# Two reorderings at the end of the couples' loop: one exponential a tanh later on ScalarE, one key product ahead of the turned gates on TensorE

## The reference

```python
# layer 2, cross attention (features = layernorm(x); textual_features = ctx)
h = jnp.tanh(txt_proj[:, None, :, :] + feat_proj[:, :, None, :] + b[None, None, :, :][..., 0, :])
rho = jnp.einsum('bftd,d->bft', h, w[:, 0])
att = jax.nn.softmax(rho + (1.0 - qm)[:, None, :] * NEG, axis=-1)
txt_h = jnp.einsum('bft,btd->bfd', att, textual_features)
w_s = jnp.tanh(jnp.einsum('bfd,od->bfo', txt_h, Wcw) + bcw)
b_s = jnp.tanh(jnp.einsum('bfd,od->bfo', txt_h, Wcb) + bcb)
x = x + jnp.tanh(g_xattn[2]) * (w_s * features + b_s)
# layer 2, experts: 16 of them, the 4 best of the 2 best groups
s = jax.nn.sigmoid(x2 @ Wg.T)
w = top4_in_best_groups(s)            # masked, normalised, times 2.5
y = y + (silu(x2 @ W1[e].T + b1[e]) * (x2 @ W3[e].T + b3[e]) @ W2[e].T + b2[e]) * w[e]
# layer 3, cross attention: keys K = ctx @ W_k.T, rotated
```

## Time and profile before

| | |
|---|---|
| median of 3 runs | 589.69 us (589.43 to 589.74) |
| profiled execution | 589.77 us, of which its span is 588.0 us |
| PE busy | 559.3 us (95%) |
| DVE busy | 441.0 us (75%) |
| ACT busy | 402.3 us (68%) |
| POOL busy | 101.9 us (17%) |
| mean granted TensorE clock | 0.994 of full speed |

### The profile page before, as it was taken

The page is one execution under the profiler, slowest core; times in us unless marked ns, Lnnn a source line. Parts: engine busy times, 40 slices in busy tenths (PEclk is TensorE's granted clock), DMA queues, the critical chain, the costliest instruction groups (busy, mean ns, idle before and its releaser), DMA issues.

```text
span 588.0 us, 8733 instructions
## 1 busy us (share of the span) xinstructions
PE 559.3 (95%) x3258; PEld 387.0 (66%) x3258; DVE 441.0 (75%) x692; ACT 402.3 (68%) x561; POOL 101.9 (17%) x69
## 2 busy tenths in 40 slices
PE   8999999898999999999996999999999999999997
PEld 5688787656767767765331346566546677888886
DVE  3377987868839799987889775766768828787786
ACT  3698899855856755426999865534504858888875
POOL 5400000000210000003999703200000310000000
PEclk8999999999999999999999899999999999999999
DMA  6118120300100369220000024506400100811100
GB/s 242 33 41 310 50 71 1 116 1 2 56 1 2 127 243 230 65 72 1 7 1 1 1 71 117 174 3 175 147 36 3 42 32 3 322 42 67 36 2 36
DMA packets 19342, 43.81 MB, mean 75 GB/s; under 512 B 2090, under 2 KB 7594, under 8 KB 19300
## 3 DMA queue, kind: packets, MB, share of 16 engines
q1 hardware_dynamic: 19300, 43.25, 22.7%
HBM read 42.55 MB, written 0.70 MB: 74 GB/s over the span
## 4 chain that ended last, share of the span: by engine, by line
PE 69%; DVE 15%; ACT 11%; issue 3%; POOL 1%; DVEq 0%; ACTq 0%; POOLq 0%
PE ps L820 36%; ACT work L1219 7%; PE ps L862 4%; PE ps L569 3%; PE ps L552 3%; DVE h_lo L1756 2%; PE ps L846 2%; PE ps L848 2%; PE ps L847 2%; PE ps L686 2%; PE ps L559 2%; PE ps L659 2%; PE ps L887 2%; PE ps L801 2%; DVE h_act L1729 2%
## 5 line engine op out<-in xcount | busy, mean ns | idle before, releaser
L1756 DVE TENSOR_TENSOR h_lo<-h_act,h_hi 128x512 fp32r<-128x512 f32 (+1 forms) x114 | 103.6, 913 | 39.7 <-ACT h_hi L1266 38.9
L820 PE MATMUL ps<-n_hi,w_hi 128*128 128x512 f32 x224 | 86.8, 422 | 2.4 <-DVE h_act L1729 1.2
L1266 ACT CAST h_hi<-h_act 128x1024 fp32r<-128x1024 f32 (+1 forms) x88 | 75.4, 857 | 14.6 <-PE ps L820 12.1
L820 PE MATMUL ps<-n_hi,w_lo 128*128 128x512 f32 x224 | 79.7, 391 | 0.0
L820 PE MATMUL ps<-n_lo,w_hi 128*128 128x512 f32 x224 | 79.6, 390 | 0.0
L1969 POOL TENSOR_TENSOR rstd<-var_eps,minus_half 128x4 f32<-128x4 f32 x16 | 17.2, 1075 | 312.1 <-DVE var_eps L1411 312.1
L1219 ACT ACTIVATE work<-work,p_rest 128x2048 f32<-128x2048 f32 x31 | 59.5, 2000 | 1.0 <-DVE work L1609 1.0
L1259 ACT ACTIVATE h_act<-ps 128x512 f32<-128x512 f32 x44 | 26.3, 598 | 45.6 <-PE ps L820 45.4
L820 PE MATMUL ps<-h_hi,w_hi 128*128 128x512 f32 x162 | 56.2, 395 | 0.1
L820 PE MATMUL ps<-h_hi,w_lo 128*128 128x512 f32 x162 | 55.3, 390 | 0.0
L820 PE MATMUL ps<-h_lo,w_hi 128*128 128x512 f32 x162 | 55.3, 390 | 0.0
(11 more groups left out here) (235 smaller groups left out, 1041.1 us busy)
## 6 DMA issues: line engine op xcount, KB each, us to landing
work<-g_rows SPq DMA_DIRECT2D x36, 512.0 KB, 5.8
w_f<-in_w SPq DMA_DIRECT2D x20, 512.0 KB, 3.7
w_f<-in_w SPq DMA_DIRECT2D x8, 384.0 KB, 3.2
work<-g_rows SPq DMA_DIRECT2D x8, 256.0 KB, 7.3
work<-g_rows SPq DMA_DIRECT2D x4, 384.0 KB, 7.2
diag<-in_w SPq DMA_DIRECT2D x2, 512.0 KB, 4.7
work<-in_w SPq DMA_DIRECT2D x2, 512.0 KB, 4.4
w_f<-in_w_rest SPq DMA_DIRECT2D x2, 384.0 KB, 4.6
```

The lines of the kernel that those rows point to most:

```text
L820: mm = pe.matmul(dst[i], wap(wt, e, lo, size, rows), mv[i], start=(first and c == 0), stop=(last and c == 2))
L1266: act.copy(places(h_hi, m, step), places(h_act, m, step)).then_inc(s["hi"], 1)
L1756: dve.tensor_tensor(lo, src, hi.bitcast(F32), ALU.subtract).then_inc(s["lo"], 1)
```

## The change

```diff
@@ TensorE, moe(m), if L == 2 @@
                         if g == 30:
                             pe.wait_ge(x2["sumA"], own_sums(2 * B - 1))
                             up(1)
+                    keep_busy(2, 4)
+                    prepare_keys(1, 1, 0)
                     turn_gates((0,))
-                    keep_busy(8, 4)
-                    prepare_keys(1, 1, 0)
                     pe.wait_ge(once["gT"], nth(m))
                     prepare_keys(1, 1, 1)
                     up(2)
@@ ScalarE, pair_sums @@
                     if g == 29:
                         norm_high(5, 0)
+                    if g == 30:
                         first_routing()
```

## The result

The changed kernel is slower: 592.11 us median of 22 runs, against 589.03 us of 22 runs of the kernel before, taken side by side on the chip. The ratio is 1.0055, with a 95% interval of 1.0045 to 1.0065, so the change costs 2.7 to 3.8 us, 3.2 in the middle. The forecast was +0.9 us, and its range ended at 591.4. (Three runs gave 589.69 us for the kernel before; over 22 it lies between 587.4 and 590.6, since TensorE's clock does not fall at the same places in every execution.)

The account below looks back on a forecast made before the run. TensorE bounds the kernel up to the last dot, then the chain over VectorE and ScalarE. 0.00 (exponential) + 0.80 (transposes) + 0.10 (clock) = 0.90 us on 589.69 gives 590.6 us; range 589.6 to 591.4.

Parts of the forecast that it names:

- Part 1: ScalarE's exponential of the logits behind tanh 29: dots gain almost nothing, later routing is covered; -0.04 to 0 us.
- Rival D: Later end of VectorE's routing holds up softmax(1) if TensorE is faster up to the last dot; +1.0 us, chance 0.02.
- Part 2: Constant matmuls and key product ahead of TensorE's transposes: they start 1.29 us later, the softmax's exponential 0.80; cost 0.80 us.
- Part 3: TensorE's clock falls at about 349, up(2) runs 1.2 us longer, waits of 1.31 us take it up; cost 0.1 us.
- Rival A: Fall of TensorE's clock not hidden, over up(3) to up(5); +1.6 us, 591.3; chance 0.20 with what else costs more.

Follow-up runs that it names:

- e1: Kernel before with only ScalarE's exponential of the logits moved behind tanh 29; ratio 0.9995, -0.3 us.
- e11: Kernel before with the later exponential of the logits, the couples' loop filled with constant matmuls, and five more ahead of the second key product; ratio 0.9994, -0.4 us.
- e2: Kernel before with only TensorE's new order: two constant matmuls and a key product ahead of the transposes, six constant matmuls gone; ratio 1.0067, +3.9 us.
- e4: Changed kernel with ten constant matmuls added between the wait for the gates' copy and the second key product; ratio 1.0020, +1.2 us.
- e8: Changed kernel with the six removed constant matmuls put back, between the wait for the gates' copy and the second key product; ratio 1.0017, +1.0 us.
- l1: Changed kernel unaltered, profiled once more; 590.19 us, with no fall of the clock around 348.
- e3: Kernel before with the eight constant matmuls behind the transposes cut to two, order unchanged; ratio 1.0011, +0.6 us.
- e13: Kernel before without the eight constant matmuls behind the transposes, order unchanged; ratio 1.0007, +0.4 us.
- e12: Changed kernel with eight instead of two constant matmuls ahead of the key product and the transposes; ratio 1.0063, +3.7 us.
- l4_before: Kernel before unaltered, profiled once more; 587.56 us, with no fall of the clock around 348.
- e6: Changed kernel with ScalarE's copy of the gates moved behind the Silu of step 0; ratio 1.0023, +1.4 us.
- e9: Changed kernel with out_bias(0) moved from between up(2) and up(3) to behind up(7); ratio 1.0063, +3.7 us.
- e10: Changed kernel with out_bias for half 0 run over all 128 rows on another operand, in the same place; ratio 1.0056, +3.3 us.
- l2: Changed kernel unaltered, a second further profile; 593.01 us, clock low from 348.6 to 358.8.
- l3: Changed kernel unaltered, a third further profile; 591.71 us, clock low from 347.8 to 358.0.

## Why the prediction was wrong

**Part 1 held, where the clock falls in the loop.** Forecast -0.04 to 0.00 us, measured 0.9995 (e1). The dots of 30 and 31 began 1.86 us before what followed them (342.99 - 341.13), against 1.89 before: 0.03 gained. Rival D, which had 0.02, named what ends this: with TensorE faster up to the last dot the later routing holds up softmax(1), for +1.0. e11's profile is that case, with +0.90.

**Part 2 held**, within 0.03 us in the profiles. The transposes came 344.29 - 342.99 = 1.30 us after the end of the dots' turn (forecast 1.29), the exponential 0.79 us later than before (0.80), and the stage without a fall grew by 0.77 to 0.80 (e2, e4, e8, l1). The key product's spacing ahead of the transposes was 344.29 - 343.43 = 0.86, the lower bound. The Trainium skill has it that TensorE drains at a change of tiling mode ("TensorEngine Tiling (Array Packing)", Key Properties). Had the 16-column transposes counted as another mode, the spacing would have been 1.06, as ahead of the dots; the trace shows no such gap between these two shapes.

**Part 3 failed, by its size.** That the clock would fall at about 349 was right in three of four profiled executions (347.8 to 348.6). The term was 0.1 us; it measured 2.6 us in the stage when the fall came (19.50 - 16.90). The step that failed is the work that was priced at the low level. I counted up(2) alone, 1.2 us more, as after a stretch like the 3.3 us of the earlier trace rows, and let TensorE's waits of 1.31 us take it up. The stretch was 10.2 us, and TensorE's work from up(2) to the mean grew by 3.90: up(2), out_bias, up(3) and most of the spread of the weights ran at 1.2 GHz. The waits took 1.31 of it, as they were to, and 2.59 were paid. With one stretch of 3.4 us the forecast is nearly right, as e3 and e13 show (+0.25 and +0.30). Rival A was this mechanism with the sign right, but also took one stretch of 3.3 us, and so ended at +1.6. Nothing in the trace of the kernel before had a low stretch longer than 3.4 us, and why this one was three times as long stays open.

**What I had not seen** is that the two costs do not add. Taking the constant matmuls away without the delay costs 0.6 us (e3), the delay with six of them behind the transposes 1.0 (e8), and both together 3.2. I counted the six as free, because TensorE idled 1.23 us ahead of up(2) anyhow. They were free as work. But the gain of taking them away was nothing, and they stood in the one place where TensorE had a serial chain of 4.79 us to sit out. e12 puts the point sharply: with eight of them ahead of the transposes the clock fell all the same.

**The chances.** Slower by over 0.2% had 0.27, within 0.2% had 0.71; it came out 0.55% slower. The base of 589.69 was the median of three like runs; over 22 runs the kernel before spreads over 3 us, so that the argument in rival D, that all executions had the same fall at 332, was drawn from too few: l4_before has its falls at 312 and 329.

## What to carry to other kernels

Ask of every constant matmul not what its time is worth but which wait it bridges. Find the serial chain over the other engines that TensorE must sit out, and count what TensorE does between the chain's start and its end; work moved ahead of the chain's first link, beyond what slack the link has (0.49 us here), delays the chain and fills nothing. Price a fall of the clock with more than one length, and with the waits that can still take up the slower work: in this stage a fall of 3.4 us added 0.3 us (e3, e13; 0.7 in e6 after its later start of 0.14), one of 6.8 us 1.6 (e12), and one of 10.2 us 2.6. And look at a cover again when the engine that gives it gets faster: part 1 cost nothing in e1 and 0.9 us in the stage of e11.

## What the runs showed of the hardware

The low stretches at this place were of three lengths: 3.4 us (e3, e6, e13), 6.8 (e9, e10, e12) and 10.2 (changed, l2, l3). In the longest TensorE had a matmul running at every moment of the last nine microseconds (349.08 to 358.1 in the changed kernel), and the clock came back only at their end. In the changed kernel it had fallen 1.2 us into an idle time of 2.40 (346.68 to 347.9), after one of 0.67 and a key product.

The same program falls at other times from one execution to the next. In the four traces of the changed kernel the first fall in the couples' loop is near 314 in three and near 320 in the fourth, and one of the four has none at 348. A single trace shows one draw; the mean granted clock that stands beside each timed run says how typical it is.
